# Swapping weights and moving operand of the degree matmuls, with five smaller changes of placement, in a graph network kernel on one core

## The reference

```
edges (src, dst): 206,250, sorted by dst, one loop a node among them
# layer 0: graph convolution, a further loop for every node
h   = relu(layernorm(x)) @ W_lin @ W_gcn
deg = segment_sum(1, dst) + 1;  dinv = deg ** -0.5
g   = segment_sum(h[src] * dinv[src] * dinv[dst], dst) + b_gcn
x   = x + relu(layernorm(g) * gamma + beta)
# layer 1: attention over the same edges, 4 heads, softmax by src
q = relu(layernorm(x)) @ Wq + bq;  k = edge_k @ Wk + bk;  v = edge_v @ Wv + bv
x = x + segment_sum(segment_softmax(q[src] . k / sqrt(32), src) * v, src) @ Wo + bo
```

## Time and profile before

| what | value |
|---|---|
| median of 3 runs | 3982.49 us (3982.22 to 3984.72) |
| the profiled execution | 3993.43 us |
| its span | 3991.7 us |
| busy: PE, PEld, DVE | 2989.5, 2139.6, 2786.9 us |
| busy: ACT, POOL | 1994.6, 1923.5 us |
| DMA | 763.92 MB, mean 191 GB/s |
| L929, the degree matmuls | 1616, busy 169.1 us |
| L553, the indirect DMAs | 1612, busy 1763.0 us |

### The profile page before, as it was taken

The page is one execution under the profiler, slowest core; times in us unless marked ns, Lnnn a source line. Parts: engine busy times, 40 slices in busy tenths (PEclk is TensorE's granted clock), DMA queues, the critical chain, the costliest instruction groups (busy, mean ns, idle before and its releaser), DMA issues. The chain is left out here.

```text
span 3991.7 us, 78472 instructions
## 1 busy us (share of the span) xinstructions
PE 2989.5 (75%) x20514; PEld 2139.6 (54%) x20514; DVE 2786.9 (70%) x6722; ACT 1994.6 (50%) x6629; POOL 1923.5 (48%) x1890
## 2 busy tenths in 40 slices
PE   3448883777777777777564778777787798999998
PEld 2227761444444444444333666666566676777777
DVE  6787776767676767676983666666666676777776
ACT  0233335666665666666222444444454565665663
POOL 2575547677676767766685555555555400000000
PEclk8555555888888888889567999999999999999999
DMA  2443334445444444544677889898898866666661
GB/s 72 149 143 109 106 101 139 156 160 172 158 158 164 160 159 163 166 152 162 192 245 222 288 290 293 283 296 286 286 299 286 266 194 200 191 190 186 190 191 33
DMA packets 512642, 763.92 MB, mean 191 GB/s; under 512 B 53960, under 2 KB 378800, under 8 KB 512430
## 3 DMA queue, kind: packets, MB, share of 16 engines
q1 hardware_dynamic: 407870, 522.25, 43.5%
q0 software_dynamic: 78160, 226.14, 15.3%
q10 hardware_dynamic: 26400, 13.11, 1.1%
HBM read 515.64 MB, written 245.65 MB: 191 GB/s over the span
## 5 line engine op out<-in xcount | busy, mean ns | idle before, releaser
L553 POOL DMA_INDIRECT table_s<-ring,place x1612 | 1763.0, 1094 | 1117.4 <-PE bank L1483 371.8
L626 ACT ACTIVATE row_base<-row_base 128x196 f32<-128x196 f32 x1414 | 496.3, 355 | 237.6 <-DVE row_base L722 218.7
L1463 PE MATMUL bank<-kT,G 128*128 128x384 f32 x1200 | 544.6, 537 | 83.0 <-ACT kT L1510 65.2
L665 ACT CAST work<-bank 128x392 bf16<-128x392 f32 x784 | 360.8, 499 | 430.0 <-remote 202.8
L960 PE MATMUL bank<-xres 128*128 128x98 bf16 x3136 | 259.5, 217 | 361.4 <-ACT work L665 210.4
L1483 PE MATMUL bank<-kv_rows,exT 128*128 128x129 f32 x3600 | 521.8, 283 | 0.0
L1554 DVE TENSOR_REDUCE gmax<-bank 128x1 f32<-128x384 f32 x600 | 331.7, 553 | 264.7 <-issue 177.2
L979 PE MATMUL bank<-parts,work 128*128 128x384 bf16 x2401 | 493.7, 363 | 0.0
L1510 ACT COPY kT<-bank 128x384 f32<-128x384 f32 x600 | 286.6, 478 | 408.2 <-PE bank L1469 244.2
L1483 PEld LDWEIGHTS bank<-kv_rows,exT 128*128 128x128 f32 x3600 | 470.2, 199 | 0.1
L1034 DVE SCALAR_TENSOR_TENSOR others<-kv_rows,node_s,iota_h 128x384 bf16<-128x384 f32 x600 | 372.1, 620 | 126.9 <-DMA kv_rows<-table_s 81.1
(11 more groups left out here) (287 smaller groups left out, 4717.8 us busy)
## 6 DMA issues: line engine op xcount, KB each, us to landing
kv_rows<-table_s SPq DMA_DIRECT2D x600, 408.0 KB
ring<-in_kv SPq DMA_DIRECT2D x402, 512.0 KB
G<-G_dram SPq DMA_DIRECT2D x600, 64.0 KB
table_s<-ring,place POOLq DMA_INDIRECT x1612
G_dram<-gst ACTq DMA_DIRECT2D x50, 256.0 KB
x_dram<-xres SPq DMA_DIRECT2D x5, 640.0 KB, 7.7
out<-ring SPq DMA_DIRECT2D x3, 1024.0 KB
table_s<-parts SPq DMA_DIRECT2D x6, 136.0 KB, 3.6
```

The costliest lines, as they stand in the source:

```text
L553: pool.indirect_dma_start(out=m["table_s"], out_offset=bass.IndirectOffsetOnAxis(ap=m["place"][0:n, i, k:k + 1], axis=0), in_=m["ring"][0: ...
L626: last = nc.scalar.activation(at, at, ACT.Identity, accum_out=m["place_f"][:, i % 2, h * STREAMS // 2 + k:h * STREAMS // 2 + k + 1])
L665: nc.scalar.copy(m["blocks"][:, t % 2, :, at:at + 4 * GN].rearrange("p h (g w) -> p g h w", w=GN), m["bank"][4 + e % 2][:, 0:4 * GW].rearr ...
L1463: pe.matmul(scores[k][:, 0:SGE], m["G"][:, u, :], m["kT"][:, k, :], start=False, stop=True, skip_group_check=True).then_inc(m["scored"], 1)
```

## The change

Six things change.

1. The degree matmul takes `hot_t` (50 columns) as weights and `hot_p` (128 columns) as the moving operand, so `hist` comes out transposed (tiles by nodes). At `DEGREES_END` DVE copies it to `hs`, PE transposes it back, and only then are `cnt` and `deg` read.
2. `POOL_STEPS` goes from (120, 136) to (112, 136): eight steps' scatters are issued in the nodes block and not in the scatter block.
3. In layer 1 a step of scatters goes with 5.75 groups and not 5, and the row loads from step 139 on are issued by POOL between its scatters, with a semaphore ring of their own, and no longer by SP.
4. `agg` is zeroed in halves by POOL and DVE.
5. The queries of odd node tiles are made by ACT (four ACTIVATE with scale and bias), those of even tiles by DVE; `q_ready` becomes a ring of two.
6. Some semaphores are merged (`wo_masked`, `mid_ready`, `mid_taken`, `counted_d`).

```diff
-POOL_STEPS = (120, 136)
+POOL_STEPS = (112, 136)
+LATE = POOL_STEPS[1] + KRING
-ROWS_EVERY = 5
-LOADS_BEHIND = 2 * ROWS_EVERY - 1
+ROWS_EVERY = 23 / 4
...
                 for x in range(HC):
-                    last = pe.matmul(hist[:, 0:NT], m["hot_p"][:, k, :, x], m["hot_t"][:, k, :, x], start=(j == 0 and x == 0), stop=True, skip_group_check=True)
+                    last = pe.matmul(hist[0:NT, 0:P], m["hot_t"][:, k, :, x], m["hot_p"][:, k, :, x], start=(j == 0 and x == 0), stop=True, skip_group_check=True)
...
                     dve.wait_ge(m["deg_summed"], HOT_STEPS)
-                    dve.tensor_copy(m["cnt"][:, 0:NT], hist[:, 0:NT]).then_inc(m["counted_d"], 1)
-                    dve.tensor_scalar(m["deg"][:, :], hist[:, 0:NT], 1.0, None, ALU.add).then_inc(m["deg_ready"], 1)
+                    dve.wait_ge(m["hw_read"], NT)
+                    dve.tensor_copy(m["hs"][0:NT, 0, :], hist[0:NT, 0:P]).then_inc(m["deg_hot"], 1)
+                    dve.wait_ge(m["deg_summed"], HOT_STEPS + 1)
+                    dve.tensor_copy(m["cnt"][:, 0:NT], hist[:, 2 * P:2 * P + NT])
+                    dve.tensor_scalar(m["deg"][:, :], hist[:, 2 * P:2 * P + NT], 1.0, None, ALU.add).then_inc(m["deg_ready"], 1)
...
                 if i == DEGREES_END:
+                    pe.wait_ge(m["deg_hot"], HOT_STEPS + 1)
+                    pe.transpose(hist[:, 2 * P:2 * P + NT], m["hs"][0:NT, 0, :], m["ident"][0:NT, 0:NT]).then_inc(m["deg_summed"], 1)
                     pe.wait_ge(m["hw_read"], NT)
-                    pe.wait_ge(m["counted_d"], 1)
+                    pe.wait_ge(m["deg_ready"], 1)
...
+            def queries(t):
+                u = t % 2
+                act.wait_ge(m["q_summed"], t + 1)
+                need(act, m["G_summed"], t - 1)
+                for h in range(HEADS):
+                    last = nc.scalar.activation(m["qm"][:, u, :, h, :], m["bank"][2 + u][:, 0:P].rearrange("d (q n) -> d q n", q=PARTS), ACT.Identity,
+                                                scale=m["qscale"][:, h:h + 1], bias=m["query_bias"][:, h:h + 1])
+                last.then_inc(m["q_ready"][u], 1)
...
-                        row, rest = divmod(r * SRING + u - LOADS_BEHIND, ROWS_EVERY)
-                        if row >= 0 and rest == 0 and POOL_STEPS[1] + KRING + row < STEPS:
-                            load_rows(m, sp, POOL_STEPS[1] + KRING + row)
...
-            pool.memset(m["agg"][:, :, :], 0.0).then_inc(m["rows_ready"], 1)
+            pool.memset(m["agg"][:, 0:HALF_TILES, :], 0.0).then_inc(m["rows_ready"], 1)
             for i in range(POOL_STEPS[1], STEPS):
                 scatter_rows(m, pool, i, ("l1_summed", ROWS_EVERY, POOL_STEPS[1]))
+                if POOL_STEPS[1] < i < STEPS - KRING + 1:
+                    load_rows(m, pool, i + KRING - 1, m["late_loaded"])
...
+            dve.memset(m["agg"][:, HALF_TILES:STILES, :], 0.0).then_inc(m["rows_ready"], 1)
             dve.memset(m["mx"][:, :], FLOOR).then_inc(m["rows_ready"], 1)
-            dve.wait_ge(m["rows_ready"], 2)
+            dve.wait_ge(m["rows_ready"], 3)
```

More of the change, by code:

```diff
@@ L118 @@
 assert TILES < KW and 4 * GW <= 512 and GROUPS_T % HC == 0 and HOTS_K % 2 == 0 and 2 * KW_NODES >= 8 + 7 and N // 8 * 8 <= N < P * P
-assert (STEPS - POOL_STEPS[1] - KRING) * ROWS_EVERY + LOADS_BEHIND <= PART_USUAL[0] and STILES % 2 == 0 and GW % 2 == 0
+assert (STEPS - POOL_STEPS[1]) * ROWS_EVERY <= PART_USUAL[0] and STILES % 2 == 0 and GW % 2 == 0
 assert NT % BATCH_T == 0 and BATCH_T >= 8 and NT - BATCH_T <= N // P < NT
@@ L521, in sent_before, with load_rows @@
     return sum(16 * columns(j) for j in range(i % KRING, min(i, STEPS), KRING))
-def load_rows(m, sp, i):
+def load_rows(m, eng, i, loaded):
     rows, u = m["kv"][0:P * W, :].rearrange("(p j) w -> p j w", j=W), i % KRING
-    need(sp, m["rows_sent"][u], sent_before(i))
+    need(eng, m["rows_sent"][u], sent_before(i))
     if i < STEPS - 1:
@@ L530, in load_rows @@
             at, n = stream(first)
-            sp.dma_start(m["ring"][:, u, first:end, 0:2 * D], rows[:, at + i:at + i + (end - first - 1) * n + 1:n, :]).then_inc(m["rows_loaded"][u], 16)
+            eng.dma_start(m["ring"][:, u, first:end, 0:2 * D], rows[:, at + i:at + i + (end - first - 1) * n + 1:n, :]).then_inc(loaded[u], 16)
     else:
         at, n = stream(SHORT)
-        sp.dma_start(m["ring"][:, u, SHORT:STREAMS - 1, 0:2 * D], rows[:, at + i:at + i + (STREAMS - SHORT - 2) * n + 1:n, :]).then_inc(m["rows_loaded"][u], 16)
-        sp.dma_start(m["ring"][0:TAIL, u, STREAMS - 1, 0:2 * D], m["kv"][P * W:E, :]).then_inc(m["rows_loaded"][u], 16)
+        eng.dma_start(m["ring"][:, u, SHORT:STREAMS - 1, 0:2 * D], rows[:, at + i:at + i + (STREAMS - SHORT - 2) * n + 1:n, :]).then_inc(loaded[u], 16)
+        eng.dma_start(m["ring"][0:TAIL, u, STREAMS - 1, 0:2 * D], m["kv"][P * W:E, :]).then_inc(loaded[u], 16)
 def scatter_rows(m, pool, i, paced):
@@ L545, in scatter_rows @@
     pool.wait_ge(m["places_ready"], i + 1)
-    pool.wait_ge(m["rows_loaded"][u], 32 * (i // KRING + 1))
+    if i < LATE:
+        pool.wait_ge(m["rows_loaded"][u], 32 * (i // KRING + 1))
+    else:
+        pool.wait_ge(m["late_loaded"][u], 32 * ((i - LATE) // KRING + 1))
     pool.wait_ge(m["keys_ready"], i + 1)
@@ L647, in parts @@
                         act.wait_ge(m["high_taken"], h + 1)
[L648 removed]
+                        nc.scalar.copy(m["parts"][:, at, 1, :], m["acc"][:, at, :]).then_inc(m["high_ready"], 1)
                     if i == SPLIT + 4 + h:
[L650 removed]
+                        act.wait_ge(m["high_taken"], h + 3)
                         nc.scalar.copy(m["parts"][:, at, 2, :], m["acc"][:, at, :]).then_inc(m["parts_ready"], 1)
@@ L1283, in queries @@
                                              m["w"]["bq"][:, 0:1], m["qscale"][:, h:h + 1], ALU.add, ALU.mult)
-                last.then_inc(m["q_ready"], 1)
+                last.then_inc(m["q_ready"][u], 1)
             for stage in range(8):
@@ L1290, in _ @@
                     normal(b, stage)
-                queries(t)
+                if t % 2 == 0:
+                    queries(t)
             dve.wait_ge(m["w12_ready"], 2)
+            dve.wait_ge(m["q_summed"], NT)
             for q in range(PARTS):
@@ L1348, in _ @@
                     turned(t + 2)
+                if t % 2 == 0:
+                    queries(t + 1)
                 if t > 0:
@@ L1364, in query @@
                 pe.wait_ge(m["h2T_ready"], t + 1)
-                need(pe, m["q_ready"], t - 1)
+                need(pe, m["q_ready"][t % 2], t // 2)
                 pe.matmul(m["bank"][6][:, t * HEADS:(t + 1) * HEADS], m["hT"][:, t % 2, :], m["bias_q"][:, :], start=True, stop=True, skip_group_check=True)
@@ L1695 @@
     l0_hot l0_summed l0_added x_padded x_ready x_stored x_reloaded
-    h2_ready h2_transposed h2T_ready q_summed q_ready G_summed G_ready
+    h2_ready h2_transposed h2T_ready q_summed G_summed G_ready
     rows_ready l1_hot k_transposed kT_ready scored reduced maxing dropped shifted max_ready
@@ L1843, in gnn_kernel @@
             m["key_bias"], m["bias_q"], m["bias_c"] = free[:, at:at + HEADS], free[:, at + HEADS:at + 2 * HEADS], free[:, at + 2 * HEADS:at + 2 * HEADS + 1]
+            m["query_bias"] = free[:, at + 3 * HEADS:at + 4 * HEADS]
             nodes_block(nc, m)
```

24 lines of the change are left out of this document (13 added, 11 removed).

## The result

The changed kernel takes 4199.78 us (median of 4; 4195.57 to 4208.6) against 3983.6 us for the kernel before in the same sitting. The ratio is 1.0534, with a 95% interval of 1.0511 to 1.0558: slower by 216 us, where +160 was forecast.

The account below looks back on a forecast made before the run. It held that no one engine bounds the kernel, whose blocks follow one another behind barriers. Terms +157 + 2 - 20 + 70 - 9 - 40 gave +160 us on 3982, so 4142 us; range 3930 to 4225, the forecast's own 4095 to 4200.

Parts of the forecast that it names:

- The degree matmuls: Degree stage: 128 strided moving columns at 1.42 ns each make a matmul 196 ns, 97 more than before, +157 us.
- The upper bound: Degree matmuls: the 99 ns are all streaming by the moving side, so 254 ns after, +250 us; chance 0.06.
- The rival of the other side: Degree stage: strided weights cost the 99 ns, moving streams freely, clock rises, DVE bounds; -55 us, 3930 us; chance 0.26.
- The two rules that the forecast cited: Degree matmuls: 16-byte SBUF lines need two hits to hide latency; fast weight load needs 128 columns, not fp32.
- The end of the degrees: After the degree matmuls: four small instructions and three hand-overs for copying and transposing back, +2 us (0 to 4).
- The scatter block: Main stage: 64 of 960 indirect DMAs leave; 11% of DVE's 179 us of remote stalls go, -20 us (0 to -50).
- The nodes block: Nodes block: POOL's 64 added DMAs, at 1.41 us a DMA, delay its end, +70 us; sharing queries is worth nothing.
- Layer 1: Layer 1: halving the memset of `agg` gives -9 us and spreading rows over 5.75 groups gives -40 us.
- The memset: Start of layer 1: zeroing `agg` in halves on POOL and DVE shortens DVE's wait, -9 us.
- at the same rate: Layer 1: a step of 5.75 groups moves 4,852 KB at the earlier byte rate, 2.93 us a group, taken as 2.95.
- the spread over 5.75 groups: Layer 1: groups beside scatters take 2.95 us each, not 3.125, -40 us (-10 to -55).
- The clock: Degree stage: the granted clock stays at 0.50, as PE is already busy 89% there and is granted no more.

Follow-up runs that it names:

- e4: Kernel before, with 16 more matmuls in twelve kinds of operand stride behind each burst of 16 degree matmuls; 3994.19 us, one run.
- e12: Kernel before, with bursts of 16 matmuls in six kinds of operand stride added in the main stage; 3813.16 us against 3833.56, one run each.
- e7: The changed kernel, still swapped, with the degree one-hots laid out in pairs (stride of 2 elements); 3744.67 us, ratio 0.9794 to the kernel before.
- e1: Kernel before with only the degree matmul swapped (and the transpose back at the end); 4055.56 us, ratio 1.0587 to the kernel before.
- e3: Kernel before with only POOL_STEPS = (112, 136), the eight steps moved; 3840.93 us, ratio 1.0035 to the kernel before.
- e5: Kernel before, unchanged, run again in the later sittings as the trace to compare stages with; 3816.79 us, one run.
- e11: The five changes without the swap, paired one-hots, but all queries on DVE; 3743.7 us, ratio 0.9774 to the kernel before.
- e10: The five changes without the swap, paired one-hots, but 5 groups a step and not 5.75; 3739.67 us, ratio 0.9766 to the kernel before.
- e8: The five changes without the swap, plus paired one-hots; 3734.53 us, ratio 0.9779 to the kernel before.
- e6: Kernel before with the degree one-hots laid out in pairs, operands not swapped; 3773.08 us, ratio 0.9859 to the kernel before.

## Why the prediction held, and where it didn't

The total came out nearer than its terms. The degrees cost 75 us more than the sum had and layer 1 gave 20 less, and the main stage gave 44 more than it had: errors of opposite sign. That the result lies within the forecast's own 4095 to 4200, by less than a microsecond, is luck; the direction is not, since the largest term had the right cause.

**The degree matmuls: the right mechanism, sized 32% too small.** "I take it that the moving side pays 1.42 ns for each strided element, whatever the clock": e4 and e12 show such a price at both clocks, and 1.8 ns. The term was 97 ns a matmul and is 136 (235 - 99), 220 us of the 232; the remaining 12 us of the stage are not broken down. What failed is the reading of the durations. A line through 96 and 392 columns was drawn down to 50 and gave 244 ns; in e4 50 contiguous columns take 217 ns, so the stride's share was 55 to 65 ns and not 28 to 38. (From its own 69 to 79 ns the forecast then took 71, 1.42 ns a column, where the middle is 74.) The other error was to split the 99 ns in 71 of streaming and 28 of load: nearly all was streaming (93 with contiguous weights). The upper bound, "the 99 ns are all streaming", 254 ns, was nearer to 235 than the 196 that was taken. The spacing was measured, in the rows; the durations, whose ends are modelled, were the weaker witness.

**The rival of the other side falls.** Strided weights cost 61 ns with 50 columns moving, not 99, and under 128 moving columns 6 ns (e12: 62 against 56 ns). With the stride gone its result comes true (e7: clock up, stage bound by DVE, 262 us; 263 was worked out), so the case hung on the layout and not on the swap.

**The two rules that the forecast cited.** The page Advanced Engine Details and Errata of the Trainium skill, section SBUF Cachelines, gives lines of 16 bytes; e12 agrees: strides of 16 and 32 bytes cost nearly the same (226 and 231 ns), 8 bytes half, 4 bytes 2 ns. That two hits on a line are enough nearly agrees at 1.2 GHz (47 against 42 ns for 50 columns) and not at 2.4 (115 against 56 for 128). The page TensorE: Matmul & The Clock Gate of the Trainium skill, section Weight-path perf modes, has the fast load of weights only with 128 columns. The trace agrees: in e4, both contiguous and at a granted clock of 0.50 (the bursts at 323.54 and 310.82 us), the load of 50 columns has a median of 163 ns and that of 128 one of 120. It hides, as the forecast had it: 106 ns with 128 contiguous moving columns is what these columns take.

**The end of the degrees.** +2 forecast, +1.4 measured.

**The scatter block.** -20 was taken within 0 to -50, and -64 came. The step "With POOL 7% less loaded in the stage I take 11% of these" failed: it priced only DVE's remote stalls, which fell by 38 us. e1 excludes a backlog, and e3 shows that the eight steps alone shorten the stage by 61 us, on chips without the remote stalls. In both pairs of traces 48 of the 64 DMAs leave this stage (744 to 696 in the first sitting, 691 to 643 from e5 to e3), and 48 at POOL's pace of 1.27 us are 61 us: their load came off whole, where the forecast said that it wouldn't "come off directly". In the first sitting POOL waited for DVE 168 us in this stage, and its last scatter came before PE's last matmul there (1884.5 against 1898.8 us), not 67 us behind it as in e5. By what link POOL's load still set the stage's length, through `selected` or the ring, wasn't tried.

**The nodes block.** 1.40 us a DMA against 1.41 taken, +69 against +70. e11 shows the queries worth nothing that can be measured, as argued.

**Layer 1.** -49 forecast, -29 measured in the first sitting and -36 to -57 in the later ones, over all pairs of runs. The memset was right (-7.7 of -9). The rest was credited to the wrong edit: "at the same rate takes 16.85 us, 2.93 us a group" gave -40 to the spread over 5.75 groups. e10 shows that the spread gives nothing measurable. The step "at the same rate" failed: with 5.75 groups a step the same 700 us (2089 to 2789) move 292 GB/s in e8, with 5 groups 298 in e10, and the groups beside scatters came at 3.08 us and not 2.95. (The byte sum also adds KB of 1,024 and of 1,000 bytes; that moves the result by less than 0.1%.) What is left over the memset, 21 us in the first sitting and 29 to 39 in the later ones (1753 to 1763 against 1716, less 7.7), goes with POOL issuing the row loads in SP's place. The forecast counted only a cost for it. PE waits less for the groups' rows with it (139 to 108 us from e5 to e10). SP, which loads the groups, no longer has row loads in its queue; that this is the link is argued from the order of its queue, not shown by a run with only that edit.

**The clock.** It stayed at 0.50 with the strided columns, as the forecast had it, though PE was busy 516 of 551 us. With the columns in pairs it was 0.68 (e6) and 0.89 (e7), though PE was busy only 176 and 205 of 260 us. What raised it isn't shown.

## What to carry to other kernels

Before swapping the operands of a matmul, look at the stride of the one that will move: in these runs (bf16) it streamed at PE's pace up to a stride of 4 bytes, and from 16 bytes on each column cost 1.8 ns, more than the matmul itself. Laying the operands out in pairs cost DVE nothing and gave more (1.4%) than the five other edits together (0.75%). When a queue sets the end of two blocks, moving its work from one to the other is a trade at the rates of the two, here 61 us for 75. And a spacing between matmuls in a row of the timeline is better evidence than the length of one.

## What the hardware showed that was not expected

The price of a strided moving operand is the same time at 1.2 and 2.4 GHz: 231 ns for 128 columns. Weights read with the same stride pay little: 62 against 56 ns under 128 moving columns (e12), 61 against 42 under 50 (e4, low clock).

The same kernel took 4% less in all the later sittings, on four chips, than in the first. In the first, DVE waits 182.7 us at L710 for remote events (a wait ended by a signal whose sender the profile of this core doesn't show) and ACT 203 us at L665; no trace of the later sittings has such waits. What they are, and whether they belong to a chip, the traces don't show.
